# One-core graph kernel: all edge weights gathered in the relation steps of half 0, and the opening up to the edge sort set out anew

## The reference

```python
x_norm = layer_norm(x, norm_g, norm_b)
out1 = gat_conv(x_norm, src, dst, W1, a_src1, a_dst1, b1, 4, 192, n)
out2 = gat_conv(out1, src, dst, W2, a_src2, a_dst2, b2, 2, 96, n)
x = layernorm(x + concat([x, out2]) @ Wu + bu)

seg = edge_type * n + dst
agg = segment_sum(x[src], seg, 34 * n)
cnt = segment_sum(ones, seg, 34 * n)
mean = agg / maximum(cnt, 1)                  # the edge weight is 1 / cnt
h1 = einsum('rni,rio->no', mean, W_rel) + x @ W_root + b_rgcn
out = gcn(h1 @ W_gcn); x = layernorm(x + out)
```

## Time and profile before

| | us |
|---|---|
| median of 3 runs | 3814.11 |
| lowest and highest | 3813.90 and 3819.71 |
| the profiled execution's own time | 3825.31 |
| its span, first to last instruction | 3823.5 |
| mean granted TensorE clock in the span | 0.927 of full speed |

### The profile page before, as it was taken

How to read it: one execution, slowest core, us unless ns; L and a number is a source line. 1 busy time by engine, 2 the same in 40 slices (tenths; PEclk the granted TensorE clock), 3 DMA queues, 4 the chain that set the end, 5 groups by cost and what they waited for, 6 DMA issues and landing times.

```text
span 3823.5 us, 59900 instructions
## 1 busy us (share of the span) xinstructions
PE 3235.7 (85%) x17157; PEld 2011.7 (53%) x17157; DVE 2262.2 (59%) x4671; ACT 1445.8 (38%) x2650; POOL 1680.9 (44%) x1418
## 2 busy tenths in 40 slices
PE   6989960039875999999999999999999998768888
PEld 3444430028863555555555566666666664434545
DVE  8999970027687445454545588787887764423224
ACT  2767710026463243333343445454554531000000
POOL 2700067730004344443441365566666535666651
PEclk9999985559987999999999999999999998889999
DMA  2010010010113333333333355554645545564441
GB/s 87 2 66 0 0 53 5 1 66 1 37 43 97 117 127 122 114 113 123 117 126 124 129 180 191 168 193 151 202 159 184 163 148 144 153 206 134 135 114 56
DMA packets 230174, 415.84 MB, mean 109 GB/s; under 512 B 36629, under 2 KB 179476, under 8 KB 230087
## 3 DMA queue, kind: packets, MB, share of 16 engines
q1 hardware_dynamic: 167840, 271.45, 20.6%
q0 software_dynamic: 60000, 141.97, 13.8%
q10 hardware_dynamic: 2246, 1.29, 0.1%
HBM read 263.22 MB, written 151.31 MB: 108 GB/s over the span
## 4 chain that ended last, share of the span: by engine, by line
PE 66%; DVE 12%; another core or an unknown queue 10%; issue 6%; ACT 2%; DVEq 2%; DMA 1%; ACTq 0%; SPq 0%; POOL 0%; POOLq 0%
PE bank L2157 15%; PE bank L2160 15%; PE bank L2159 15%; PE bank L2146 5%; PE bank L2042 3%; DVE arena L1434 3%; PE bank L2322 2%; PE bank L1985 2%; PE bank L2133 2%; PE bank L2134 2%; PE bank L2333 2%; PE bank L1913 1%; PE bank L1888 1%; DVE arena L1433 1%
## 5 line engine op out<-in xcount | busy, mean ns | idle before, releaser
L2157 PE MATMUL bank<-arena 128*128 128x384 f16 x3675 | 1202.6, 327 | 29.6 <-DVE arena L1698 15.1
L2159 PE MATMUL bank<-arena 128*128 128x384 f16 x3675 | 1201.4, 327 | 2.3 <-issue 2.3
L2160 PE MATMUL bank<-arena 128*128 128x384 f16 x3675 | 1201.1, 327 | 2.3 <-issue 2.3
L1150 ACT ACTIVATE arena<-bank,winv 128x384 f32<-128x384 f32 x700 | 399.3, 579 | 947.3 <-PE bank L2160 820.5
L1698 DVE SCALAR_TENSOR_TENSOR arena<-bank,winv,arena 128x384 f32<-128x384 f32 x525 | 316.5, 613 | 434.8 <-PE bank L2160 404.3
L2157 PEld LDWEIGHTS bank<-arena 128*128 128x128 f16 x3675 | 360.5, 98 | 288.3 <-issue 23.2
L2160 PEld LDWEIGHTS bank<-arena 128*128 128x128 f16 x3675 | 360.4, 98 | 240.0 <-issue 4.0
L2159 PEld LDWEIGHTS bank<-arena 128*128 128x128 f16 x3675 | 360.8, 98 | 237.3 <-issue 11.7
L771 POOL DMA_INDIRECT arena<-y_half,idx_now x360 | 398.3, 1106 | 189.9 <-issue 104.4
L1591 DVE SCALAR_TENSOR_TENSOR arena<-arena,wscale 128x1152 f16<-128x1152 f32 x245 | 366.5, 1531 | 165.1 <-ACT arena L1073 157.2
L785 POOL DMA_INDIRECT arena<-y_half,idx_now x360 | 345.2, 959 | 189.0 <-issue 104.4
(11 more groups left out here) (244 smaller groups left out, 4312.5 us busy)
## 6 DMA issues: line engine op xcount, KB each, us to landing
y_half<-arena SPq DMA_DIRECT2D x306, 384.0 KB
arena<-in_L_gnn_W_rel_dram SPq DMA_DIRECT2D x68, 1152.0 KB, 9.6
arena<-y_half,idx_now POOLq DMA_INDIRECT x720
y_half<-arena SPq DMA_DIRECT2D x34, 294.0 KB
cT_dram<-arena SPq DMA_DIRECT2D x1, 5625.0 KB
arena<-cT_dram SPq DMA_DIRECT2D x9, 625.0 KB
arena<-in_x_dram SPq DMA_DIRECT2D x10, 384.0 KB
typ_s<-rel_inv_dram,idx_w POOLq DMA_INDIRECT x240
```

The lines of the kernel that those rows point to most:

```text
L1150: nc.scalar.activation(y[half][:, :, c * CQ:(c + 1) * CQ], acc, ACT.Copy, scale=scale).then_inc(r_copied, 1)
L2157: nc.tensor.matmul(acc, h, w_hi[m - 1][:, k, :], start=fresh and k == 0, stop=False, skip_group_check=True)
L2159: nc.tensor.matmul(acc, h, w_lo[m - 1][:, k, :], start=False, stop=False, skip_group_check=True)
L2160: ins = nc.tensor.matmul(acc, l, w_hi[m - 1][:, k, :], start=False, stop=k == KH - 1, skip_group_check=True)
```

## The change

1. `EARLY` is gone. The 240 gathers in one run are removed; each of 15 relation steps of half 0 gathers all six of its units, 24 gathers instead of 8. `w_now` is widened to six units. POOL's copies are removed; ACT copies 24 columns of indices in (`indices_in`) and 24 columns of weights out (`weights_out`), once per step, and POOL waits for the first of these.
2. In the opening DVE takes x in three groups (4, 4 and 2 tiles), as PSUM banks are filled, makes scale and shift, and ACT applies them (one ACTIVATE per tile). DVE's ten scaling instructions are gone, and its first edge work lies between the statistics.
3. `gcol`, `bcol`, `a1s` and `a1d` are loaded by SP's queue behind x, and ACT waits for the two columns alone. ACT runs one square root early, which loads its table.
4. PE sums the counts ahead of all half products instead of after two. `place` raises `units_ready` by itself, so POOL's scatter does not wait for the buckets of the units.
5. `SCAT` is 90: 90 scatters, and 240 columns in 16 parts through PE.

```diff
-        w_now = sb("w_now", [P, 2, UT], F32)
+        w_now = sb("w_now", [P, IDXB, UT], F32)
-        SCAT = 75
+        SCAT = 90
-        EARLY = 60
-        LATE = (UNITS - EARLY) // AGG_PAIRS
...
+            with nc.allow_non_contiguous_dma(reason="short vectors, a few hundred elements"):
+                sp.dma_start(gcol[:, :], col(norm_g)).then_inc(col_loaded, 16)
+                sp.dma_start(bcol[:, :], col(norm_b)).then_inc(col_loaded, 16)
             sp.dma_start(W1s[:, :, 0:D], W1.rearrange("(k p) o -> p k o", p=P)).then_inc(w1_loaded, 16)
+            sp.dma_start(a1s, a_src1.rearrange("h c -> (h c)").partition_broadcast(P)).then_inc(vec_loaded, 16)
+            sp.dma_start(a1d, a_dst1.rearrange("h c -> (h c)").partition_broadcast(P)).then_inc(vec_loaded, 16)
...
-            for e in range(EARLY):
-                if e >= 2:
-                    for t in range(UT):
-                        pool.wait_ge(g_loaded[e % 2 * UT + t], e // 2 * 16)
-                pool.nop(nofuse=True)
-                for t in range(UT):
-                    k = e * UT + t
-                    nc.gpsimd.indirect_dma_start(
-                        out=w_s[:, k:k + 1], out_offset=None, in_=w_dram,
...
                 t4(q, i)
-                for c in range(LATE):
-                    weigh(i, c)
-                    if c:
-                        weighed(i, c - 1)
-                weighed(i, LATE - 1)
-                pool.wait_ge(edge_w, i * LATE + LATE)
+                pool.wait_ge(idx_copied, i + 1)
+                pool.nop(nofuse=True)
+                for c in range(4):
+                    weigh(c)
                 t3(next_q, next_i)
+                weigh(4)
                 t1_t2(next_q, next_i)
+                weigh(5)
...
+            nc.scalar.activation(credit[:, 0:1], epsc[:, 0:1], ACT.Sqrt)
+            for g, (a, b) in enumerate(X_GROUPS):
+                act.wait_ge(var_ready, b)
+                nc.scalar.activation(sd[:, a:b], mv[:, a:b, 1], ACT.Sqrt, bias=epsc[:, 0:1]).then_inc(std_ready, 1)
+                act.wait_ge(rstd_ready, g + 1)
+                for n in range(a, b):
+                    r = rows(n)
+                    nc.scalar.activation(xs[0:r, n, :], xs[0:r, n, :], ACT.Identity, bias=shift[0:r, n:n + 1],
+                                         scale=rstd[0:r, n:n + 1]).then_inc(xn_ready, 1)
...
                 m1_out(s, 1)
+                if w is not None:
+                    weights_out(w)
+                if w is not None and q == 0 and (not isinstance(i, int) or i < AGG_PAIRS):
+                    indices_in(w + 1)
                 m7_out(s, 0)
...
+            x_stats(range(0, 4))
+            x_stats(range(4, 5))
+            x_scale(0)
+            x_stats(range(5, 6))
             dve.wait_ge(idx_loaded, 48)
...
+            x_stats(range(6, 8))
...
+            bucket(range(0, 1))
+            x_scale(1)
+            x_stats(range(8, NT))
+            bucket(range(1, 2))
+            x_scale(2)
+            bucket(range(2, NT))
```

More of the change, by code:

```diff
@@ L385, in program @@
         H_BANK, HB = 3, 3
-        H_EARLY = 2
+        X_GROUPS = [(a // P, cdiv(b, P)) for a, b in NBANKS]
         H_FIRST = NT
@@ L455, in program @@
         assert UT % FREE == 0
-        assert UNITS % IDXB == 0 and PER % IDXB == 0
+        assert UNITS % IDXB == 0 and PER == IDXB and PER % 2 == 0
         spread = [bank[0][:, 0:P], bank[SUMS][:, 0:P]]
@@ L1307, in _ @@
             after(nc.vector.tensor_copy(iota[:, :], iota_i))
-            for n in range(NT):
-                r = rows(n)
-                if n % XP == 0:
-                    dve.wait_ge(x_loaded[n // XP], 16 * (XP if n + XP >= NT else 1))
-                nc.vector.bn_stats(stats[0:r, n, 0:6], xs[0:r, n, 0:D // 2])
-                after(nc.vector.bn_stats(stats[0:r, n, 6:12], xs[0:r, n, D // 2:D]))
-                nc.vector.bn_aggr(mv[0:r, n, :], stats[0:r, n, :]).then_inc(var_ready, 1)
-            dve.wait_ge(std_ready, 1)
@@ L1317, in _, with x_stats @@
-            after(nc.vector.reciprocal(rstd[:, :], sd[:, :]))
-            for n in range(NT):
-                r = rows(n)
-                nc.vector.tensor_scalar(xs[0:r, n, :], xs[0:r, n, :], mv[0:r, n, 0:1], rstd[0:r, n:n + 1],
-                                        ALU.subtract, ALU.mult).then_inc(xn_ready, 1)
+            def x_stats(ns):
+                for n in ns:
+                    r = rows(n)
+                    if n % XP == 0:
+                        dve.wait_ge(x_loaded[n // XP], 16 * (XP if n + XP >= NT else 1))
+                    nc.vector.bn_stats(stats[0:r, n, 0:6], xs[0:r, n, 0:D // 2])
+                    after(nc.vector.bn_stats(stats[0:r, n, 6:12], xs[0:r, n, D // 2:D]))
+                    nc.vector.bn_aggr(mv[0:r, n, :], stats[0:r, n, :]).then_inc(var_ready, 1)
@@ new lines, in x_scale, with bucket @@
+            def x_scale(g):
+                a, b = X_GROUPS[g]
+                dve.wait_ge(std_ready, g + 1)
+                dve.wait_ge(var_ready, b)
+                after(nc.vector.reciprocal(rstd[:, a:b], sd[:, a:b]))
+                nc.vector.scalar_tensor_tensor(shift[:, a:b], mv[:, a:b, 0], -1.0, rstd[:, a:b], ALU.mult,
+                                               ALU.mult).then_inc(rstd_ready, 1)
+            def bucket(ks):
+                for k in ks:
+                    after(nc.vector.tensor_scalar(ohb[:, k, :], dbk_f, float(k), None, ALU.is_equal))
+                    after(nc.vector.tensor_tensor_scan(scan[:, k, :], ones_e, ohb[:, k, :], 0.0, ALU.mult, ALU.add))
@@ L1878, in _ @@
                     ins.then_inc(xnT_psum, 1)
+            pe.wait_ge(part_tot, 1)
+            nc.tensor.matmul(bank[6][0:EP, 0:NT], tri[0:EP, 0:EP], small[0:EP, 0:NT], start=True, stop=True)
+            nc.tensor.matmul(bank[6][:, NT:2 * NT], ones[0:EP, :], small[0:EP, 0:NT], start=True,
+                             stop=True).then_inc(sort_psum, 1)
             pe.wait_ge(xnT_ready, len(NBANKS) * KT)
@@ L1895, in _ @@
             pe.wait_ge(w1_loaded, 16)
-            for i in range(H_EARLY):
-                h_product(i)
-            pe.wait_ge(part_tot, 1)
-            nc.tensor.matmul(bank[6][0:EP, 0:NT], tri[0:EP, 0:EP], small[0:EP, 0:NT], start=True, stop=True)
-            nc.tensor.matmul(bank[6][:, NT:2 * NT], ones[0:EP, :], small[0:EP, 0:NT], start=True,
-                             stop=True).then_inc(part_psum, 1)
-            for i in range(H_EARLY, H_FIRST):
+            for i in range(H_FIRST):
                 h_product(i)
```

88 lines of the change are left out of this document (38 added, 50 removed).

## The result

The changed kernel takes 3695.31 us (median of 4 runs, 3693.56 to 3698.68) against 3816.91 us before (4 runs): a ratio of 0.9674 with a 95% interval of 0.9657 to 0.9691, 122 us less. The forecast was 3535 us with a range to 3595 us, so the direction is right and the size is off by 160 us.

What follows compares the result with a forecast made beforehand. PE was taken to be held by POOL's 240 early gathers and to bound the relation steps. -270 - 14 + 5 = -279 us from 3823.5 us, plus 1.8 us around it, less 11.2 us to the median: 3535 us, range 3515 to 3595 us.

Steps and rivals of the forecast that it cites:

- The hole: Stretch before the softmax where TensorE is nearly idle beside POOL's 240 early gathers; removing them was to save 270 us.
- rival B: PE is slow in the idle stretch for its own reason, so that stretch stays: 3805 us, chance 0.11.
- The opening: From the start to the sort's end: less DVE work and more scatters end it at 208 us, 14 us less.
- the two paths said to meet: At the sort's end, DVE's chain with PE's tail and the scatters with SP's load both end near 208 us.
- The steps of half 0: Half 0's 15 relation steps, 24 gathers each instead of 8: 5 us more in all, ceiling 90 us.
- The POOL overrun: In half 0's steps, gathers at 1.62 us exceed POOL's 1.6 us slack: 6 us a step, 90 us ceiling.
- rival D: Gathers hold PE wherever they stand, so half 0's steps lose too; slower, 4130 us if held whole; chance 0.04.
- A: The forecast case: the gathers hold PE and the idle stretch closes, 3535 us, spanning 3518 to 3565 us; chance 0.76.

Runs made afterwards that it cites:

- a_none: Changed kernel with its 360 weight gathers left out, POOL zeroing the columns by small memsets and waits changed to fit: 3537.09 us (ratio 0.9239).
- b_spaced: Kernel before, with two small memsets and waits on POOL behind each gather of the long run of 240: 3674.17 us (ratio 0.9602).
- a_again: The changed kernel itself, unaltered, run again in a later group: 3442.83 us against 3454.26 us for the kernel before (ratio 0.9962).
- run 147: Not a run's label: in the long run of 240 early gathers in the kernel before, 147 matmuls went through; that kernel took 3816.91 us.
- a_nops: Changed kernel with one empty TensorE instruction more for every third matmul of the relation steps, 105 a step: 3442.43, 3442.11 and 3442.99 us.
- b_direct: Kernel before with plain POOL DMAs in place of its 240 early gathers: 3460.77, 3459.36, 3461.34 and 3459.34 us.
- c_mixed: Changed kernel with 120 gathers in an early run, two memsets behind each, and 16 per step as 8, 4, 4: 3443.35, 3442.73, 3442.80 us.
- a_split: Changed kernel with a step's 24 gathers laid out in three rows of 8 instead of 16, 4, 4: 3590.88 us (ratio 0.9381).

## Why the prediction was wrong

*The hole* (-270 us) was right as to place, cause and size. L1510 starts at 551.1 us; the forecast was 565 less 14. From the earlier trace rows that is 283.8 us, of which 271 us are the hole and 13 us the opening. That the gathers hold TensorE, and not something of TensorE's own (rival B), is shown by a_none, which differs from the changed kernel in POOL's gathers and the waits for them alone, and by b_spaced, which changes nothing but what stands between them. It holds for the holding chip: on the free chips there is no hole to close, and the forecast did not know that.

*The opening* (-14 us) was right to a microsecond: the columns of the edges are joined at 208.74 us, against 221.73 us before. In the timeline of the changed kernel, DVE's `part_tot`, its answer, its place, the sort's first column, and the join:

```profile
36.45 0.17 DVE L1351 COPY small<-arena 125x10 f32<-125x10 f32 x1
...
41.72 0.17 DVE L1364 TENSOR_SCALAR smalli<-bank 128x10 int32<-128x10 f32 x1
...
55.81 0.25 DVE L1381 SCALAR_TENSOR_TENSOR arena<-arena 125x90 int32<-125x90 f32 x1
...
73.56 0.32 DVE L1411 TENSOR_SCALAR arena<-iota,arena 125x128 f16<-125x128 f16 x1 [0.32 <-issue]
...
208.74 0.53 DVE L1419 SCALAR_TENSOR_TENSOR idx_y<-bank,arena 128x360 int32<-128x360 f32 x1 [8.64 <-DMA arena<-placed_dram]
```

Forecast were 37, 42.2, 56.5, 74.4 and 208 us. The wait of 8.64 us is for SP's load of the scattered edges, so of the two paths said to meet it is the scatters' that ends last. ACT's scaling, guessed at 0.85 us, takes 0.95 us a tile and costs nothing; `gcol` and `bcol` were in time (ACT's copies out of PSUM start at 28.45 us).

*The steps of half 0* (+5 us, ceiling 90 us) is the step that failed: they cost 158 us, 153 us more than the term. I let 24 gathers cost what half 1's row shows, 0.163 us a matmul. That row has 24 gathers too, but they wait there for VectorE and for the sums, at most four to eight in a row, and 16 in a row at 1.25 us stood in no step. The long run was the nearest row, not half 1's. I had read from it that TensorE keeps its pace for the first 28 us, which was wrong too: with 147 matmuls and 33 gathers it keeps it for 47 us, until small gaps with no named releaser begin at 538.30 us. And I did not ask whether a busier TensorE has less time: at six matmuls in a microsecond it had 12.4 us, 10 gathers and 77 matmuls. The POOL overrun that set my ceiling didn't occur: POOL waits 11.48 us ahead of the next `t4`. So the range left out what rival D described, that the gathers hold TensorE in the steps too. D's sign was wrong because its price was: 158 us for the 240 gathers that were moved is 0.66 us each, not over 1.18 us. Even half 1's row was not free of the holding, as the 19 us of a_again show.

*The rest of the 160 us.* The term accounts for 154 us by the traces. I took 11.2 us off because the profiled execution of the kernel before was that much above its median, while the changed kernel's was 1.75 us below its own: 13 us. Half 1 and what follows took 7 us less than before, which nothing in the change explains and no run was made for. The bounds were also added up wrongly: with hole 250 to 275 us, opening 6 to 16 us and steps 0 to 15 us, A alone spans 3523 to 3573 us, not 3518 to 3565 us. The measured 3695 us lies outside either.

*Rival B's rule.* The Trainium skill, page "SBUF — State Buffer", section "Who interferes with whom", says "PE and ACT never wait on anyone". The free chips agree with it: in a_again a step with 24 gathers takes 52.1 us. On the holding chip TensorE stops in 14 of the 15 steps with gathers, and with the gathers left out in none of these, so there the measurement is against the sentence, though none of the runs shows that SBUF is what TensorE waits for.

*What stays open.* What in a gather holds TensorE, and why in the result and one group and not in the five others. The holding chip's records show no slower transfers: 1.25 us from gather to gather and DMA engines at 1 to 2% in the stop, and between 1008 and 1879 us, where the steps loop, no instructions are loaded through the DMA queues. An emptied buffer of instructions would fit that TensorE alone stops and, in the steps, at the same matmul, but not by itself that in the long run 147 matmuls went through and not 77; a_nops was to tell, and never met a holding chip. Nor did b_direct or c_mixed, so the best version shown there that computes everything is a_split, 3590.88 us; on the free chips a_again and c_mixed are equal.

## What to carry to other kernels

A row of small indirect gathers from POOL can hold TensorE where POOL's own time is not short, and in these runs the price fell when something stood between them: POOL's other work behind every eighth (54 us in place of 158 us, so eight in a row are not free either), or two memsets behind each. Where a run has time, stretch it, and then see what else stood behind it on POOL. When a stall has a known cause, and the change moves that cause to where its victim has no slack, price it by the row in which it did harm, not by the mildest. And a gain of 3% that a chip with the stall shows may be 0.4% on one without; run the kernel before beside every group.

## What the runs showed of the hardware

The same program took 3828 us in one group and 3454 to 3457 us in five others, steadily within each group to 0.5%. In the two traces of the changed kernel all but 2 us of the difference lie beside indirect gathers. On the holding chip 240 gathers at 1.30 us cost some 270 us, a row of 16 at 1.25 us about 11 us a step, three rows of 8 3.7 us a step, and 360 row gathers in the tail 73 us; a run at 1.63 us or more, and 75 or 90 scatters at 1.6 us, cost nothing that can be seen. The instructions of VectorE, ScalarE and POOL in the steps took as long as on a free chip (POOL's gather 0.95 us and 0.94 us, ScalarE's L1141 0.58 us in both), and the granted clock fell to 1.2 GHz only after TensorE had stood still (1.00 from 1350 to 1354 us with TensorE busy for 0.95 us, then 0.50).
